# First attention stage: merged bias products, 64-column masks, maxima two units further ahead, rows turned inside a split value run

## The reference

```python
q, k, v = (x @ W.T + b  for each), split into 16 heads of 8 features
sim = einsum('bhid,bhjd->bhij', q, k)
sim = sim + bias[h, i - j] * SCALE        # a learned bias, constant for i - j >= 113
sim = where(j > i, -inf, sim)             # causal
out = softmax(sim) @ v ; out = out @ Wo.T + bo
```

## Time and profile before

| | |
|---|---|
| median of 3 runs | 1803.59 us (1802.31 to 1805.47) |
| the profiled execution's own time | 1807.43 us |
| its span, first to last instruction | 1805.7 us |
| busy in the span | PE 91%, DVE 83%, ACT 70%, PEld 58%, POOL 43% |
| first attention, `rows(0)` to `rows(63)` | 72.7 to 486.0 us |
| mean granted TensorE clock | 0.945 |

### The profile page before, as it was taken

The page is one execution under the profiler, slowest core; times in us unless marked ns, Lnnn a source line. Parts: engine busy times, 40 slices in busy tenths (PEclk is TensorE's granted clock), DMA queues, the critical chain, the costliest instruction groups (busy, mean ns, idle before and its releaser), DMA issues. The chain is left out here.

```text
span 1805.7 us, 48183 instructions
## 1 busy us (share of the span) xinstructions
PE 1639.5 (91%) x19082; PEld 1047.6 (58%) x19082; DVE 1503.7 (83%) x2238; ACT 1255.6 (70%) x2481; POOL 783.7 (43%) x1501
## 2 busy tenths in 40 slices
PE   5599999999976999999999649999999999999965
PEld 3366666676665877877677423444444444444544
DVE  7699999999766999987555669999999999999835
ACT  6488888888843444454333537898898989898955
POOL 5488888888835010000000233444444444444446
PEclk9699999999966999999999877999999999999978
DMA  7522232323162566653000161111121121112021
GB/s 246 202 80 85 88 95 85 94 87 94 57 138 57 95 89 95 91 89 54 1 1 0 70 250 38 59 52 60 53 72 52 59 67 57 55 58 68 28 75 47
DMA packets 119908, 141.86 MB, mean 79 GB/s; under 512 B 22221, under 2 KB 80778, under 8 KB 119690
## 3 DMA queue, kind: packets, MB, share of 16 engines
q1 hardware_dynamic: 119258, 138.79, 29.9%
q10 hardware_dynamic: 432, 0.07, 0.0%
HBM read 92.70 MB, written 44.98 MB: 76 GB/s over the span
## 5 line engine op out<-in xcount | busy, mean ns | idle before, releaser
L887 DVE TENSOR_REDUCE heads_mx<-heads_psM 128x1 f32<-128x1024 f32 x512 | 602.1, 1219 | 48.3 <-PE heads_psM L978 32.0
L958 ACT ACTIVATE heads_probs<-heads_psS 128x512 f32<-128x512 f32 x1024 | 546.0, 600 | 77.2 <-PE heads_psS L1001 71.2
L927 POOL TENSOR_TENSOR heads_masked<-heads_probs,g_tri 128x128 f32<-128x128 f32 x512 | 234.4, 458 | 359.3 <-ACT heads_probs L958 359.2
L653 POOL TENSOR_TENSOR heads_probs<-heads_probs,one_ebias 128x256 f32<-128x256 f32 (+1 forms) x512 | 342.6, 696 | 77.9 <-ACT heads_probs L685 77.5
L614 DVE TENSOR_REDUCE heads_mx<-heads_psM 128x1 f32<-128x1024 f32 (+7 forms) x512 | 349.5, 749 | 24.9 <-PE heads_psM L696 23.1
L685 ACT ACTIVATE heads_probs<-heads_psS 128x512 f32<-128x512 f32 x576 | 316.2, 602 | 69.5 <-PE heads_psS L696 64.2
L978 PE MATMUL heads_psM<-three_kS,three_qS 48*128 48x512 bf16 x1024 | 230.1, 394 | 20.9 <-PEq L1969 12.1
L1001 PE MATMUL heads_psS<-three_qS,three_kS 50*128 50x512 bf16 x1024 | 237.7, 388 | 0.7 <-ACT heads_probs L958 0.3
L1509 ACT ACTIVATE trees_hid_hi<-trees_hid 128x512 fp32r<-128x512 f32 x192 | 121.7, 634 | 152.4 <-DVE trees_hid L1530 151.3
L1530 DVE SCALAR_TENSOR_TENSOR trees_hid<-trees_psH,g_b,trees_chosen 128x512 f32<-128x512 f32 x192 | 143.8, 749 | 32.4 <-DMA trees_chosen<-leaf_choice 15.3
L1026 PE MATMUL heads_psO<-heads_probs,heads_ones_only 128*32 128x128 f32 x1920 | 162.0, 284 | 0.0
(11 more groups left out here) (253 smaller groups left out, 3134.4 us busy)
## 6 DMA issues: line engine op xcount, KB each, us to landing
trees_chosen<-leaf_choice SPq DMA_DIRECT2D x96, 256.0 KB, 7.3
head_outputs<-g_small SPq DMA_DIRECT2D x128, 128.0 KB
one_qS<-q_parts SPq DMA_DIRECT2D x128, 96.0 KB
one_kS<-k_parts SPq DMA_DIRECT2D x128, 96.0 KB
three_qS<-q_parts SPq DMA_DIRECT2D x128, 96.0 KB
three_kS<-k_parts SPq DMA_DIRECT2D x128, 96.0 KB
q_parts<-g_w SPq DMA_DIRECT2D x8, 768.0 KB, 4.5
k_parts<-g_w SPq DMA_DIRECT2D x8, 768.0 KB, 6.0
```

The lines of the kernel that those rows point to most:

```text
L653: pool.tensor_tensor(pr[:, a:a + w], pr[:, a:a + w], bass.AP(eb.tensor, eb.offset + NEAR - 1, [list(eb.ap[0]), [-1, w]]), ALU.mult).then_i ...
L887: dve.tensor_reduce(mx[:, n % 2, k:k + 1], psM[k % 2][:, :], AXX, ALU.max, negate=True).then_inc(max_taken, 1)
L927: pool.tensor_tensor(masked[n % 2][:, kb, :], probs[n % 2][:, kb, kb * P:(kb + 1) * P], g["tri"][:, 0:P], ALU.mult).then_inc(near_done, 1)
L958: act.activation(probs[n % 2][:, kb, h * CH:(h + 1) * CH], ring.bank(i)[:, :], ACT.Exp).then_inc(slot_taken, 1)
```

## The change

- GpSimd multiplies in five products a head and not eight: blocks (0, 1), (2, 3) and (5, 4) together, 512 columns each, 7 and 6 alone (`NEARS`, `weight`).
- The reductions on VectorE give the negative of the maximum at once (`negate=True`), and the rounding moves to GpSimd (`minus_maxima`): a copy to bf16 and a subtraction, behind the fourth of its products.
- A mask is two products of 64 columns and not of 128: for each half of the mask's columns, a bf16 table of 64 rows by 128 columns as weights and one of 64 by 64 moving. Two tables in place of three, built by 14 selections, each of which waits for the one before, and one DMA in place of two.
- `maxima` issues first the products of all its blocks, in turn in the two banks, then the masks.
- TensorE runs two more units of maxima ahead: `maxima(n + 2, 2)` and `(n + 2, 3)` behind `scores(n, 1)`, `(n + 2, 4)` behind `scores(n, 4)`, `(n + 3, 0)` behind `scores(n, 6)`, `(n + 3, 1)` behind `scores(n, 8)`; `maxima(2, 0)` and `(2, 1)` stand ahead of the loop.
- The values run in four parts. The first stands ahead of `rows(n + 1)`, the second right behind it. The first waits for four of GpSimd's five products, the third for all.

```diff
@@ -211,9 +214,8 @@
...
-                sp.wait_ge(made, 10)
-                for half in (0, HALF):
-                    sp.dma_start(g["masks"][HALF - half:P - half, 1, :, :], g["masks"][half:half + HALF, 0, :, :]).then_inc(masks_swapped, 16)
+                sp.wait_ge(masked, MASK_STEPS)
+                sp.dma_start(g["masks"][HALF:P, :, :], g["masks"][0:HALF, :, :]).then_inc(masks_copied, 16)
...
@@ -304,16 +306,36 @@
...
-                for table, op, fill, sign in ((0, ALU.not_equal, 1.0, -1), (1, ALU.is_ge, NEG, -1), (2, ALU.is_ge, NEG, 1)):
-                    t = g["masks"][:, 0, table, :]
-                    pool.affine_select(out=t, in_=t, compare_op=op, fill=fill, base=0, pattern=[[sign, P]], channel_multiplier=-sign).then_inc(made, 1)
...
+                def choose(table, at, width, op, fill, base, step, down):
+
+                    t = g["masks"][0:HALF, table, at:at + width]
+                    pool.affine_select(out=t, in_=t, compare_op=op, fill=fill, base=base, pattern=[[step, width]],
+                                       channel_multiplier=down).then_inc(masked, 1)
+                    masks_made[0] += 1
+                    pool.wait_ge(masked, masks_made[0])
+
+                masks_made = [0]
...
+                    choose(table, 0, P, ALU.not_equal, 1.0, 0, -1, 1)
+                    choose(table, P, P, ALU.not_equal, 1.0, HALF, -1, 1)
+                    alone = (last - 1, -1) if last else (-1, 1)
...
 
@@ -516,13 +538,13 @@
     ORDER = [0, 1, 2, 3, ROWS, 4, 5, 6, 7, 8]
     MAXIMA = [(7,), (0, 6), (1, 5), (2, 4), (3,)]
     NM = len(MAXIMA)
-    NEAR_ORDER = [0, 1, 7, 2, 6, 3, 5, 4]
-    NEAR_AFTER = [0, 2, 3, 4, 5, 6, 7, 8]
-    VALUES = [[(0, 0), (1, 0), (2, 0), (3, 0), (0, 1), (1, 1), (2, 1), (3, 1), (0, 2), (1, 2), (2, 3), (3, 4), (0, 3)],
-              [(0, 4), (1, 3), (2, 2), (3, 2), (0, 5), (1, 4)],
-              [(0, 6), (1, 5), (2, 4), (3, 3), (0, 7), (1, 6), (2, 5)]]
-
-    ENDS = VALUES[2][-4:]
+    NEARS = [((0, 1), 2), ((7,), 3), ((6,), 5), ((2, 3), 6), ((5, 4), 8)]
+    NEAR_FIRST = 4
+    VALUES = [[(0, 0), (1, 0), (2, 0), (3, 0), (0, 1), (1, 1)], [(2, 1), (3, 1), (0, 2)],
+              [(1, 2), (2, 2), (3, 2), (0, 3), (1, 3), (2, 3), (3, 4), (0, 4), (1, 4), (0, 5)],
+              [(2, 4), (3, 3), (0, 6), (1, 5), (2, 5), (0, 7), (1, 6)]]
+
+    ENDS = [(3, 3), (2, 5), (0, 7), (1, 6)]
 
     def place(kb, qb):
 
@@ -611,19 +633,12 @@
...
-                        last = dve.tensor_reduce(mx[:, p, qb:qb + 1], psM[(n * NM + i) % 2][:, at:at + w], AXX, ALU.max)
+                        last = dve.tensor_reduce(mx[:, p, qb:qb + 1], psM[(n * NM + i) % 2][:, at:at + w], AXX, ALU.max, negate=True)
...
-                dve.wait_ge(max_taken, (n + 1) * NM)
-                dve.wait_ge(block_taken, (n + 1) * (TPB - NM))
-                if n >= 2:
-
-                    dve.wait_ge(slot_done, ring.rows(n - 2) + 1)
-                dve.tensor_scalar(nm[:, p, 0, :], mx[:, p, :], -1.0, None, ALU.mult).then_inc(nm_hi, 1)
-                dve.wait_ge(nm_hi, n + 1)
...
+
             for b in range(B - 1):
...
@@ -643,15 +658,35 @@
...
+            def minus_maxima(n):
+
+                p = n % 2
+                pool.wait_ge(max_taken, (n + 1) * NM)
+                pool.wait_ge(block_taken, (n + 1) * (TPB - NM))
+                if n >= 2:
+                    pool.wait_ge(slot_done, ring.rows(n - 2) + 1)
+                pool.tensor_copy(nm[:, p, 0, :], mx[:, p, :]).then_inc(nm_hi, 1)
+                pool.wait_ge(nm_hi, n + 1)
+                pool.tensor_tensor(nm[:, p, 1, :], mx[:, p, :], nm[:, p, 0, :], ALU.subtract).then_inc(nm_ready, 1)
+
+            def weight(n, blocks):
+
+                pr, eb, w = probs[n % 2][:, :], g["ebias"][:, n % HEADS, :], near_width(blocks[0])
+                a = place(blocks[0], blocks[0])
+                step = place(blocks[-1], blocks[-1]) - a
+                at = bass.AP(pr.tensor, a, [list(pr.ap[0]), [step, len(blocks)], [1, w]])
+                by = bass.AP(eb.tensor, eb.offset + NEAR - 1, [list(eb.ap[0]), [0, len(blocks)], [-1, w]])
+                pool.tensor_tensor(at, at, by, ALU.mult).then_inc(near_done, 1)
+
             stage_v(0)
+            minus_maxima(0)
+            minus_maxima(1)
             for n in range(NG):
-                pr = probs[n % 2]
-                for kb, unit in zip(NEAR_ORDER, NEAR_AFTER):
+                for blocks, unit in NEARS:
                     pool.wait_ge(slot_taken, ring.index(n, unit) + 1)
-                    a, w = place(kb, kb), near_width(kb)
-                    eb = g["ebias"][:, n % HEADS, :]
-                    pool.tensor_tensor(pr[:, a:a + w], pr[:, a:a + w], bass.AP(eb.tensor, eb.offset + NEAR - 1, [list(eb.ap[0]), [-1, w]]),
-                                       ALU.mult).then_inc(near_done, 1)
+                    weight(n, blocks)
+                    if unit == NEARS[-2][1] and n + 2 < NG:
+                        minus_maxima(n + 2)
                 if n + 1 < NG:
                     stage_v(n + 1)
 
@@ -690,10 +725,12 @@
 
         @block.tensor
         def _(pe):
-            def mask(out, r, table):
-
-                for s in range(2):
-                    done = pe.matmul(out, g["masks"][r:r + HALF, s, 0, :], g["masks"][r:r + HALF, s, table, :], start=False, stop=s == 1)
+            def mask(out, r, table, stop=True):
+
+                m2 = g["masks"][r:r + HALF, table, :]
+                for half in range(2):
+                    done = pe.matmul(out[:, half * HALF:(half + 1) * HALF], m2[:, half * P:(half + 1) * P], m2[:, 2 * P:2 * P + HALF],
+                                     start=False, stop=stop and half == 1)
                 return done
 
             def maxima(n, i):
@@ -707,18 +744,28 @@
...
-                at = 0
+                runs, ends, at = ([], []), [], 0
                 for qb in MAXIMA[i]:
                     w = (qb + 1) * P
                     for bank in range(2):
                         a, z = max(at, bank * CH), min(at + w, (bank + 1) * CH)
-                        if a >= z:
-                            continue
-                        r, ends = HALF * bank, z == at + w
-                        last = pe.matmul(ps[:, a:z], qS[u][r:r + PROWS, qb * P:(qb + 1) * P], kS[u][r:r + PROWS, a - at:z - at], start=True, stop=not ends)
-                        if ends:
-                            last = mask(ps[:, z - P:z], r, 1)
+                        if a < z:
+                            runs[bank].append((qb, a, z, a - at))
                     at += w
+                    ends.append(at)
+                for j in range(max(len(of) for of in runs)):
+                    for bank in range(2):
+                        if j < len(runs[bank]):
+                            qb, a, z, first = runs[bank][j]
+                            r = HALF * bank
+                            pe.matmul(ps[:, a:z], qS[u][r:r + PROWS, qb * P:(qb + 1) * P], kS[u][r:r + PROWS, first:first + z - a],
+                                      start=j == 0, stop=j + 1 == len(runs[bank]) and (bank + 1) * CH not in [-(-e // CH) * CH for e in ends])
+                for half in range(2):
+                    for z in ends:
+                        r, at = HALF * ((z - 1) // CH), z - P + half * HALF
+                        m2, later = g["masks"][r:r + HALF, 0, :], [e for e in ends if z < e <= -(-z // CH) * CH]
+                        last = pe.matmul(ps[:, at:at + HALF], m2[:, half * P:(half + 1) * P], m2[:, 2 * P:2 * P + HALF], start=False,
+                                         stop=half == 1 and not later)
                 last.then_inc(maxima_done, 1)
 
             def rows(n):
@@ -756,9 +803,11 @@
...
                 if part == 0:
                     pe.wait_ge(v_staged, n + 1)
-                    pe.wait_ge(near_done, (n + 1) * TPB)
+                    pe.wait_ge(near_done, n * len(NEARS) + NEAR_FIRST)
                     if n > 0:
                         pe.wait_ge(o_taken, n)
+                if part == 2:
+                    pe.wait_ge(near_done, (n + 1) * len(NEARS))
                 pr, v = probs[n % 2][:, :], v_ones[n % 3]
                 for c, kb in VALUES[part]:
                     out = psO[c * VW:(c + 1) * VW, 0:2 * P]
@@ -779,28 +828,32 @@
...
                 maxima(1, i)
+            maxima(2, 0)
+            maxima(2, 1)
             for n in range(NG):
                 scores(n, 0)
                 scores(n, 1)
-                maxima(n + 2, 0)
-                maxima(n + 2, 1)
+                maxima(n + 2, 2)
+                maxima(n + 2, 3)
                 scores(n, 2)
                 scores(n, 3)
                 values(n - 1, 0)
                 rows(n + 1)
+                values(n - 1, 1)
                 scores(n, 4)
-                maxima(n + 2, 2)
+                maxima(n + 2, 4)
                 scores(n, 5)
                 scores(n, 6)
-                maxima(n + 2, 3)
-                values(n - 1, 1)
```

(18 more changed lines are left out.)

15 lines of the change are left out of this document (13 added, 2 removed).

## The result

The changed kernel takes 1788.59 us (median of 5 runs, 1785.70 to 1793.69), the kernel before, run on the same chip, 1803.42 (1802.02 to 1805.47). The ratio is 0.992, 95% interval 0.9902 to 0.9939: faster by 14.8 us, where 20.6 were forecast (from 1803.59 to 1783). The time lies inside the range and inside the narrower one of the forecast's own case (1773 to 1796).

The account below looks back on a forecast made before the run. Two limits were taken: TensorE's 6.28 us a head and the often longer chain through the `mrow` DMAs. A gain of 0.365 us over 62 heads, 22.6, less 2.0 at the start gave 1783 us from 1803.6; range 1768 to 1804.

Parts of the forecast that it names:

- case 5: Whole kernel: the forecast itself, 1783 us, with its own range of 1773 to 1796; chance 0.62.
- The chain to the copy's end: Score 0 through exponentials and `rows` to the copy's end: shortened by 0.29 to 2.98 us, limited by ScalarE.
- The floor: TensorE's need in a head whose DMA is on time: falls by 0.57, to 5.70 us.
- The mask's price of 0.03 us: TensorE's mask products: 64 columns take about 0.03 us, since bf16 loads already fit into 0.055.
- rival 1: TensorE's masks: weight loads set their pace, so TensorE needs 6.10 us and the time is 1792; chance 0.14.
- TensorE's own work needs 6.28 us: Kernel before, a head on time: TensorE's work takes 6.28 us, one of two limits beside the DMA chain.
- VectorE 6.12: Kernel before: eight reductions of 5.42 us and rounding make 6.12 us a head, about as little room as TensorE.
- Rival 4: GpSimd's merged products cost half again, 1.9 for 1.27 us, and GpSimd becomes the bound: slower, 1849; chance 0.12.
- Maxima ahead: Maxima two units ahead: new waits of about 0.1 us a head at 5.70, and 2 us once at the start.
- with half of each: 0.365 a head: The sum: late heads gain 0.29 us, heads on time 0.44; half of each takes 6.50 to 6.13.
- rival 3: SP's queue: the DMAs land later by what the chain gained, 0.37, so no gain, 1804 to 1806; chance 0.07.
- the four loads and the store ahead of the two DMAs in the same turn: SP's queue: a shorter head brings these closer to the `mrow` DMAs, which could then land later by 0.37 us.

Follow-up runs that it names:

- e5_rows_behind: Changed kernel with `rows` behind the second part of the values instead of ahead of it: 1792.81 us, 0.9941 of the kernel before.
- e1_masks128: Changed kernel with masks of 128 columns again, all else as changed: 1796.83 us, 0.9954 of the kernel before.
- e10_before_store_behind: Kernel before with only the store of outputs moved behind the two `mrow` DMAs: 1795.49 us, 0.9949 of the kernel before.
- e6_round_vector: Changed kernel with the rounding of the maxima back on VectorE, all else as changed: 1806.02 us, 1.002 of the kernel before.
- e12_maxima_not_ahead: Changed kernel with maxima in their old places and the rounding behind GpSimd's last product: 1789.16 us, 0.9912 of the kernel before.
- e2_light_loads: Changed kernel with q and k loads cut to 64 of 1024 columns from head 6 on: 1762.67 us, 0.9776 of the kernel before.
- e4_store_behind: Changed kernel with the store of outputs issued behind the two `mrow` DMAs: 1771.57 us, 0.9818 of the kernel before.

## Why the prediction was right, and where its sizes were off

*The mechanism* was that of the forecast, case 5: two limits, the chain through the `mrow` DMAs and the engines' floor, and both came down. That the time fell well inside the range is in part luck: sizes too low and too high stand against each other below.

*The chain to the copy's end.* Forecast 2.98 us, measured 2.92: ScalarE's exponentials limit it, and L700 starts right behind the fourth. The late head gained 0.33 for 0.29. In `e5_rows_behind` `rows` starts 2.41 us behind score 0 and not 2.19, and the copy's end stays nearly where it is (2.93): what ScalarE does sets it, as the step said. It also means that the split of the values was not needed for this; with `rows` behind nine entries in place of 13 the copy is already as early. Before, `rows` started at 2.73 and the copy waited for it.

*The floor.* Forecast 5.70, measured 5.78. The mask's price of 0.03 us, taken from bf16 pairs and not from the f32 loads of L1351, held; rival 1 (6.10) is out. The forecast read L1351 without its clock: from 516 to 518 us the trace of before has 0.50, so the 0.23 us were measured at 1.2 GHz and said less for rival 1 than it took them for. `e1_masks128` shows that the masks are worth 0.37 of floor.

The Trainium skill in TensorE: Matmul & The Clock Gate (LDWEIGHTS) gives a load as its columns divided by 1.2, an estimate of 107 ns for 128; if products waited for their loads, the masks would have kept their price. Here a mask's load does last 0.09 to 0.10 us by its own record (L732 on PEld at 301.62 and 301.80), but the two masks start 0.03 apart, so the load runs beside other work. The same page of the Trainium skill (Wait — 56ns, not 53.3ns?) gives a product as its columns at 2.4 GHz and 2.5 ns, an estimate of 29 ns for 64, with which the row agrees.

*A step that was wrong without hurting the sum: "TensorE's own work needs 6.28 us", and VectorE 6.12.* VectorE's round of 6.28 has no gap over 0.04 us (`e10_before_store_behind`). The second rounding step, 0.17, and the steps between were left out of the 6.12. The floor of the new order with the old masks is 6.15 (`e1_masks128`); what TensorE needed in the old order no run shows. So the floor was VectorE's at least as much as TensorE's, and the change took 0.8 us from VectorE's by moving the rounding. The forecast costed that move as room for GpSimd alone; `e6_round_vector` shows it as the part without which nothing is gained: 17 us.

*GpSimd.* Merged 1.273 us (forecast 1.27), rounding 0.193 + 0.201 (0.191 + 0.202), in all 86.58% of 6.25 = 5.41 us a head (5.3). Rival 4 is out: a pattern that jumps and runs backwards takes what L326 took, 1.27 us.

*Maxima ahead.* The wait for VectorE is 0.12 us a head (forecast 0.1). The start cost 2.3 us (2), but that the numbers meet is luck. Head by head it is 2.3 more in the first, 1.3 less in the second, 2.0 more in the third and 0.7 less in the fourth. The third is the one with the clock, which rose at 96.4 us and at 90.8 before. In the eight other kernels with the maxima ahead and a clock that rose by 93 us, `rows(0)` to `rows(4)` takes 30.1 to 31.0, where before took 30.3 and the kernel without the maxima ahead (`e12_maxima_not_ahead`) 27.8. So the place of the maxima costs 2.3 to 3.2 us at the start, nearly all of it in the first head (10.2 to 10.7 us for 7.6 to 8.0).

*The term that was mis-sized: where the DMAs land.* The sum took them as before in every head ("with half of each: 0.365 a head") and left a later landing to rival 3, as all or nothing, with 0.07. It came true in part. An estimate takes for each head the larger of the floor, 5.78, and of copy, landing and 0.05 us to score 0 (2.92 + landing + 0.05). With the landings of the trace of before the mean head is 6.08 us, 0.41 less than before; measured, with the mean landing 0.16 later, it is 6.25, 0.24 less. So the later landings cost 0.17 a head, and 0.045 of it is hidden because the forecast's own 0.365 was that much too low. What is left is 62 x (0.365 - 0.24) = 7.8 us short; the result is 5.8 short, and the 2 between them lie within the scatter of what is behind the stage.

The forecast even named the place ("the four loads and the store ahead of the two DMAs in the same turn") but put no size to it. It could have: in the trace of before 47 of 56 heads had the store 1.8 us ahead, and the nine with less landed at 3.2 to 4.4 and not at 2.9. SP's order says the same, with numbers of the trace of before: 4.44 us of issues and an output 1.85 us ahead of the copy's end are 6.29, the old floor, so every shorter head pushes the store towards the DMAs. `e2_light_loads` and `e4_store_behind` show the cost by taking one neighbour away each; from `e10_before_store_behind` to `e4_store_behind`, with the store out of the way in both, the change brings 24 us, more than was forecast.

What stays open is how the loads and the store together make a given head late, and why some land late even with the store behind (up to 4.4 us).

## What to carry to other kernels

When a latency chain that contains a DMA is shortened, price what stands ahead of that DMA in its queue: group the heads of the trace by the distance from the neighbour's issue to the DMA's, and read the landing in each group. A large store that nobody waits for belongs behind a small DMA on which the next round depends; here two swapped statements were worth 17 us behind a change that had brought 15, and 9 us ahead of it. And where two engines show 97%, look at both timelines for gaps before a floor is put down to one of them. When an edit seems to show in a trace, look for the same step in the traces of kernels that lack the edit, and at the clock of both: the 2.7 us at the start were not the edit's.

## What the runs showed of the hardware

- An operation of VectorE on 8 columns that starts while a product of GpSimd runs ends only when the product has ended. Alone L624 takes 171 ns and L647 168; the medians are 698 (before) and 701 (`e6_round_vector`):

```profile
L624 DVE TENSOR_SCALAR heads_nm<-heads_mx x64: 171/698/709, 72.3 to 483.9; 128x8 bf16<-128x8 f32 x64
```
```profile
L647 DVE TENSOR_TENSOR heads_nm<-heads_mx,heads_nm x64: 168/701/706, 70.7 to 485.0; 128x8 bf16<-128x8 f32 x64
```

  In both traces only the operations that overlap with nothing on GpSimd (one, and two) are at the least. The 63 others of L624 end 25 to 32 ns behind the end of the product beside them, the 62 others of L647 21 to 25 ns. The second step before, L626, takes 0.17 us in every head: it starts when that product is over, and the next begins at most 0.11 us before its end; the CAST of L645 takes 0.17 too, and in 60 of 64 heads the next product of GpSimd starts 12 to 18 ns before it ends. So what such an operation costs is what is left of the product. GPSIMD Engine Reference of the Trainium skill (Specifications) says that GpSimd shares VectorE's interfaces to SBUF and contends with VectorE's operations that have two inputs there or run in a two-port mode; the trace agrees for the subtraction with its two inputs, 0.70. On GpSimd itself the same rounding costs 0.19 and 0.20.
- The second of two DMAs of 4 KB lands between 2.4 and 4.8 us behind the copy that both wait for (before and after), and what stands ahead of them in the queue decides much of it: on average 2.86 us with the store 1.57 us ahead, 4.50 with it under 1.0.
- In one head of the changed kernel TensorE waits 1.79 us for the `mrow` DMA, until 332.07 us. The granted clock of 330 to 335 us is 0.70 (the row above), so part of it ran at 1.2 GHz (332.0 to 335.4), and the head takes 8.84 us, the longest of all: a late landing can cost twice.
